# Five more edge groups of a graph kernel sorted in its first stage (60 of 202 instead of 55), two in every second block

## The reference

```python
# L0: twice
agg = segment_sum(x[src], dst) / max(count, 1)
h = relu(agg @ W_l + b_l + x @ W_r)
# then
x = layernorm(x + h @ W_out + b_out)
# L1: over the edges
out = concatenate([x[src], edge_attr], axis=1)           # 206250 x 128
out = selu(out @ W1a + b1a) @ W1b + b1b
mean = segment_sum(out, dst) / max(count, 1)
h = concatenate([x, mean, u[batch]], axis=1)
x = layernorm(x + selu(h @ W2a + b2a) @ W2b + b2b)
```

## Time and profile before

| | us |
|---|---|
| median of 3 runs | 3514.62 |
| lowest, highest | 3498.83, 3517.24 |
| profiled execution | 3513.92 |
| its span, first to last instruction | 3512.1 |
| mean granted TensorE clock | 0.782 |

### The profile page before, as it was taken

The page is one execution under the profiler, slowest core; times in us unless marked ns, Lnnn a source line. Parts: engine busy times, 40 slices in busy tenths (PEclk is TensorE's granted clock), DMA queues, the critical chain, the costliest instruction groups (busy, mean ns, idle before and its releaser), DMA issues.

```text
span 3512.1 us, 52018 instructions
## 1 busy us (share of the span) xinstructions
PE 2340.6 (67%) x18382; PEld 1666.3 (47%) x18382; DVE 1547.9 (44%) x3098; ACT 1005.2 (29%) x2255; POOL 1824.9 (52%) x1853
## 2 busy tenths in 40 slices
PE   3999999787888862565656566565656656564643
PEld 1555565444444431454544455454545545453543
DVE  6899998233333441333433333343333334332333
ACT  4778776000000011222222222222222222222222
POOL 6366763555455557454444545444554544455552
PEclk9999999888888875677777777777767777676566
DMA  6658877649455521322222222222222222221111
GB/s 227 196 196 241 224 210 253 175 119 219 143 173 176 176 68 40 83 48 44 46 48 43 48 46 48 44 46 48 43 48 46 48 44 46 48 42 42 39 37 34
DMA packets 478172, 346.45 MB, mean 99 GB/s; under 512 B 357844, under 2 KB 428687, under 8 KB 474253
## 3 DMA queue, kind: packets, MB, share of 16 engines
q1 hardware_dynamic: 367443, 272.49, 27.4%
q0 software_dynamic: 54240, 57.23, 7.5%
q10 hardware_dynamic: 56250, 13.52, 1.9%
HBM read 200.58 MB, written 142.39 MB: 98 GB/s over the span
## 4 chain that ended last, share of the span: by engine, by line
PE 36%; another core or an unknown queue 25%; issue 22%; DVE 6%; ACT 5%; DMA 2%; SPq 2%; DVEq 1%; ACTq 1%; POOL 0%; POOLq 0%
PE agg_ps L1533 5%; PE u_ps L1664 4%; PE cnt_ps L1404 4%; PE cnt_ps L1625 3%; PE agg_ps L1410 3%; PE agg_ps L1411 3%; PE u_ps L1660 2%; PE agg_ps L1674 2%; PE agg_ps L1633 2%; ACT A_sb L1071 2%; PE t_ps L1617 1%; PE v_ps L1650 1%; DVEq L2192 1%; ACT A_sb L1217 1%
## 5 line engine op out<-in xcount | busy, mean ns | idle before, releaser
L976 POOL DMA_INDIRECT A_sb<-source_terms,src_cur x1172 | 1118.5, 954 | 1048.4 <-ACT src_cur L1203 718.1
L927 POOL DMA_INDIRECT sorted_edges<-pm_row,pm_to x440 | 482.7, 1097 | 338.8 <-DVE pm_to L1981 215.5
L1664 PE MATMUL u_ps<-arena 128*128 128x64 bf16 x3399 | 253.4, 212 | 385.5 <-issue 385.2
L1533 PE MATMUL agg_ps<-A_sb,arena 128*128 128x448 f16 x1911 | 426.1, 373 | 68.7 <-issue 65.7
L1857 DVE TENSOR_TENSOR arena<-iota_code,arena 128x2048 f16<-128x2048 f16 (+1 forms) x392 | 438.3, 1186 | 33.5 <-PE cnt_ps L1404 31.2
L1071 ACT ACTIVATE A_sb<-cnt_ps 128x392 f32 (+1 forms) x784 | 386.0, 499 | 123.4 <-PE cnt_ps L1404 73.0
L1664 PEld LDWEIGHTS u_ps<-arena 128*128 128x128 bf16 x3399 | 196.7, 110 | 439.9 <-issue 431.9
L2194 DVE TENSOR_TENSOR A_sb<-A_sb,agg_ps 65x48 f32 (+1 forms) x290 | 78.0, 269 | 728.7 <-remote 624.4
L1533 PEld LDWEIGHTS agg_ps<-A_sb,arena 128*128 128x128 bf16 x1911 | 189.5, 101 | 274.0 <-issue 133.0
L1404 PE MATMUL cnt_ps<-arena 128*128 128x98 f16 x3136 | 282.2, 214 | 31.2 <-ACT A_sb L1071 23.2
L1633 PE MATMUL agg_ps<-A_sb 128*65 128x48 f32 x2344 | 210.9, 250 | 131.4 <-issue 73.4
(11 more groups left out here) (308 smaller groups left out, 3379.3 us busy)
## 6 DMA issues: line engine op xcount, KB each, us to landing
counts_matrix<-A_sb SPq DMA_DIRECT2D x14, 5488.0 KB
A_sb<-counts_matrix SPq DMA_DIRECT2D x12, 5488.0 KB
arena<-in_edge_attr_dram SPq DMA_DIRECT2D x96, 256.0 KB
sorted_edges<-zrow SPq DMA_DIRECT2D x11, 1716.0 KB
A_sb<-source_terms,src_cur POOLq DMA_INDIRECT x1172
arena<-sorted_edges SPq DMA_DIRECT2D x143, 128.0 KB
overlapping_rows<-A_sb SPq DMA_DIRECT2D x1, 13056.0 KB, 39.4
A_sb<-in_edge_attr_dram SPq DMA_DIRECT2D x50, 256.0 KB
```

Of the source, the lines that this page charges most:

```text
L927: pool.indirect_dma_start(out=sorted_d, out_offset=bass.IndirectOffsetOnAxis(ap=pm_to[:, k, j:j + 1], axis=0), in_=pm_row[:, k, j, :], in_ ...
L976: pool.indirect_dma_start(out=gath[k][:, j * F:(j + 1) * F], out_offset=None, in_=p_d, in_offset=bass.IndirectOffsetOnAxis(ap=src_cur[k][: ...
L1533: ins = pe.matmul(agg_ps[:, 0:SBN], Hsb[:, part, blk, :], Asb(half)[:, blk, :], start=False, stop=(part == 2), skip_group_check=True)
L1664: ins = pe.matmul(u_ps[:, j * F:(j + 1) * F], lane_p[u % 2][:, a, j * P:(j + 1) * P], P3[:, 2 * b + a, part, :], start=False, stop=(part = ...
```

## The change

`NR` goes from 11 to 12: 12 ranges, 60 sorted groups, 156 units, 142 conventional groups. `IN_STAGE1` goes from 10 to 15: blocks 4, 6, 8, 10 and 12 (`TWO_SORTS`) sort two groups each, blocks 3, 5, 7, 9 and 11 one. The second group of a block is started on VectorE when the one-hots up to group 32 are made and the first group's slots are found; TensorE places it after group 32 (the first after 16), and its slots are found when the one-hots up to group 48 are made. SyncE loads the groups a block ahead, so two in a block ahead of a double one. Three ranges are cleared before block 2 instead of two; the nine later clears stay where they were. GpSimd waits for all three before the first scatter. `LAST_STEP` goes from 121 to 116, so the 156 + 3 steps of units lie in slots 4 to 115: 47 slots with two, 65 with one. The last 26 slots are as before. The number of groups sorted between the stages and in stage 2 is the same, 5 and 40, at the same places. The units' products stay in three bf16 parts.

```diff
--- before.py
+++ after.py
@@ -69,7 +69,7 @@
 DEEP = 6
 
 RG = 5
-NR = 11
+NR = 12
 PG = RG * NR
 NEGC = NEG - PG
 CELL = 2 * P
@@ -80,10 +80,11 @@
 BEFORE = 3 * (NSB - 1) + 3 - PG
 UNIT_RING = 3
 FIRST_SORT = 3
-IN_STAGE1 = 10
+TWO_SORTS = (4, 6, 8, 10, 12)
+IN_STAGE1 = 10 + len(TWO_SORTS)
 SOONER = IN_STAGE1 + 5
-PLACE_AT = 16
-SLOT_AT = 32
+PLACE_AT = (16, 32)
+SLOT_AT = (32, 48)
 TOTALS = 4 * -(-NEG // 4)
 
 
@@ -112,7 +113,7 @@
 UNIT_RANGE = [r for r, tiles in enumerate(CELL_TILES) for _ in range(sum(tiles) // UT)]
 STEPS = UNITS + 3
 FIRST_STEP = 4
-LAST_STEP = 121
+LAST_STEP = NEGC - 26
 
 FIN_SLOT = LAST_STEP + 1
 FIN_ORDER = list(range(4, 12)) + [0, 1, 2, 3] + list(range(12, NSB))
@@ -533,10 +534,13 @@
             eng.wait_ge(row_stored, 16 * (NSB + 1))
 
         def placed(q):
-            return cnt_ps[q % 2][:, 0:NCELL] if IN_STAGE1 <= q < SOONER else t_ps[:, SBN:SBN + NCELL]
+            return cnt_ps[(q - IN_STAGE1) % 2][:, 0:NCELL] if IN_STAGE1 <= q < SOONER else t_ps[:, SBN:SBN + NCELL]
 
         def sorted_in(s):
-            return [s - FIRST_SORT] if FIRST_SORT <= s < FIRST_SORT + IN_STAGE1 else []
+            if not FIRST_SORT <= s < NSB - 1:
+                return []
+            first = s - FIRST_SORT + sum(t < s for t in TWO_SORTS)
+            return [first, first + 1] if s in TWO_SORTS else [first]
 
         def fin_stage(h, stage):
             n = h - FIN_SLOT - stage
@@ -600,9 +604,12 @@
                     sp.dma_start(xm[:, 1 - half, :, :], by_node(x, s - 1)).then_inc(xm_in[1 - half], 16)
                 if s >= 2:
                     store_h(s - 2, half)
-                    load_group(s - 2)
+                    for q in sorted_in(s + 1):
+                        load_group(q)
+                if s == NSB - 2:
+                    load_group(IN_STAGE1)
                 if s == NSB - 1:
-                    for q in range(s - 1, IN_STAGE1 + PRING):
+                    for q in range(IN_STAGE1 + 1, IN_STAGE1 + PRING):
                         load_group(q)
                 sp.wait_ge(counts_moved, (s + 1) * SB_GROUPS + 2)
                 sp.dma_start(A_d[bass.ds(s, 1), :, :].rearrange("a p n -> (a p) n"), A_sb[:, half, :]).then_inc(A_stored[half], 16)
@@ -617,15 +624,15 @@
                 sp.dma_start(pm_dst[:, :], dst[0:PG * EG].rearrange("(r q) -> r q", q=RG * EG)[:, 0].partition_broadcast(P)).then_inc(pm_dst_in, 16)
             superblock(0, 0)
             superblock(1, 1)
-            for r in range(2):
+            for r in range(IN_STAGE1 // RG):
                 blank(r)
             for s in range(2, NSB):
                 superblock(s, s % 2)
                 if s >= FIRST_SORT + 1:
                     if s == FIRST_SORT + 1:
                         sp.wait_ge(pm_gone[0], 16 * EJ)
-                    if s - FIRST_SORT + 1 < NR:
-                        blank(s - FIRST_SORT + 1)
+                    if s - FIRST_SORT - 1 + IN_STAGE1 // RG < NR:
+                        blank(s - FIRST_SORT - 1 + IN_STAGE1 // RG)
             sp.wait_ge(xT_ready, NSB - 2)
 
             def last_rows(rows, done):
@@ -934,7 +941,7 @@
                     gather_fine((m + 3) * SETS, (m + 4) * SETS)
                 split_h(m - 2)
                 if m == FIRST_SORT:
-                    pool.wait_ge(pm_blank, PM_BLANK + 32)
+                    pool.wait_ge(pm_blank, PM_BLANK + 16 * (IN_STAGE1 // RG))
                 for q in sorted_in(m):
                     scatter(q)
             pool.wait_ge(rows_ready, NSB)
@@ -1420,8 +1427,8 @@
                         turn_first(1)
                     if k == (LATE_TURN if known and s == 0 else 3 * BG) - 1 and (not known or s < NSB - 1):
                         turn_windows(s + 1)
-                    if k == PLACE_AT:
-                        for q in sorted_in(s):
+                    for q, at in zip(sorted_in(s), PLACE_AT):
+                        if k == at:
                             place_group(q)
                     if known and s == 0:
                         continue
@@ -1880,15 +1887,16 @@
                 if not known or s < NSB - 2:
                     dve.wait_ge(fine_in, 16 * SETS * (s + 3))
                     find_windows(s + 2)
-                for q in sorted_in(s):
+                for q, at in zip(sorted_in(s), SLOT_AT):
                     sort_group(q)
-                    make_hot(s, half, begun, SLOT_AT)
-                    begun = SLOT_AT
-                    own_terms(s - 2)
+                    make_hot(s, half, begun, at)
+                    begun = at
+                    if at == SLOT_AT[0]:
+                        own_terms(s - 2)
                     slot_group(q)
                 if s >= 2 and not sorted_in(s):
-                    make_hot(s, half, begun, SLOT_AT)
-                    begun = SLOT_AT
+                    make_hot(s, half, begun, SLOT_AT[0])
+                    begun = SLOT_AT[0]
                     own_terms(s - 2)
                 make_hot(s, half, begun, SB_GROUPS)
 

```

## The result

The kernel after takes 3641.4 us (median of 4 runs, 3630.3 to 3650.7) against 3515.9 for the kernel before beside it: 1.036 times, 95% interval 1.030 to 1.042. That is slower, by 125 us, and outside the predicted range of 3500 to 3553. Its profiled execution has a span of 3647.4 us, 135.3 more than the one of before.

| stretch | before | after | change | forecast |
|---|---|---|---|---|
| start to the end of counting (stage 1) | 602.3 | 658.0 | +55.7 | +23 |
| from there to slot 4 (stage 2 and what joins on) | 798.8 | 794.5 | -4.3 | 0 |
| slots with units (117, 112) | 1793.4 | 1887.5 | +94.1 | -10 in all of stage 3 |
| the last slots and the end | 317.7 | 307.5 | -10.2 | |

A forecast was written before the change was run, and what follows sets the result against it. It took TensorE and VectorE to bound stage 1 together, and stops with no engine full to mark stage 3. From 3513.9 us, +14 (sorts), +9 (clear) and -10 (stage 3) gave 3527 us, range 3500 to 3553.

The forecast's parts named there:

- (b): Stage 1, SyncE's queue: a third clear before block 2 delays the load of `xm` and adds 9 us, bounds 0 to 10.1.
- (a): Stage 1, VectorE: a second sort makes each double block 3.0 us longer, 14 us in all, bounds 10.6 to 19.3.
- (c): Stage 1, GpSimd: eight more scatters per double block take 15.7 us and fit in 16.4 us of waiting per pair.
- Cost 0: Stage 1, GpSimd: the added scatters, with later windows and a later split of h, were to add no time.
- Rival 2: Stage 1: runs of 16 scatters stop the engines, up to 25 us, so 3552 us; chance 0.2.
- added nothing: Stage 1, block 2: no time was charged for what a longer wait for `xm` does to the granted clock.
- I take the stops as a cost of the gathers, so of the conventional groups: Stage 3: engine stops, 53% of the chain or 8.1 us a slot, were charged to conventional groups, not units.
- b: Stage 3: time of one unit, 3.3 us, beside a, a slot without its units, 11.3; change -5a + 13b = -13.6.
- My way by slots: Stage 3: double slots of 18.6 us and single ones of 14.3 gave +5.9 us, a second unit costing 4.3.
- two ways that charged a slot with 11.3 and 12.0: Stage 3: splits by the chain and by the slots without units, giving changes of -13.6 and -24.6 us.
- rival 3: Stage 3: the stops belong to units, so it changes by +38 us and the kernel takes 3575; chance 0.05.
- No engine is full there: Stage 3, slots with units: GpSimd, the busiest but TensorE, has only 884.71 of 1793.41 us of work.

The follow-up runs named there:

- after_again: The kernel after, run once more unchanged, on a chip without stops: 2615.1 us against 2632.5 for the kernel before, ratio 0.9924.
- sort_doubles: The kernel after without the second groups' scatters in stage 1 and with the 47 double slots first, on a chip with stops: 3495.4 us against 3486.2 for the kernel before.
- scatter_only: The kernel before with 8 more scatters into a scratch table in blocks 4, 6, 8, 10 and 12, on a chip without stops: 2639.0 us against 2638.2.
- paused forms: Kernels before and after with seven small memsets behind each group's gathers in stage 3 (before also paused in stage 2): unit slots 1716.7 and 1753.0 us.
- before_paused: The kernel before with seven small memsets behind every group's gathers in stage 3, on a chip with stops: 3329.3 us against 3486.2, ratio 0.956.
- two_two: The kernel after with its double slots in pairs (2 2 1 1 1) instead of alternating, on a chip without stops: unit slots 1123.3 us.

## Why the prediction was wrong

**Right.** (b), the clear: 9 us forecast, 8.7 measured (14 by the base of another chip). (a), VectorE: double blocks of 41.6 forecast; 41.0 to 42.5 in after_again, and 41.6, 41.6, 42.8, 41.5 and 45.9 in sort_doubles. (c) in its sum: 40 scatters cost GpSimd's own time nothing. Beside VectorE's one-hots a scatter did take longer: of the 55 of scatter_only between 255 and 525 us, the 44 that lay mostly beside one took 1.69 us on average, the 11 others 0.96. Where no stop disturbs, stage 1 grew by 25.0 us, and by 32.6 on another chip, against 23. Stage 2: none, and measured -4 and 0.

**Stage 1, wrong by 33 us.** The step that failed is "Cost 0" in (c). Rival 2 named the cause, runs of 16 scatters; I priced it with stage 2's 5.1 us a block in five blocks and gave it 0.2. The scatters alone, on a chip with stops, cost 36 us. They don't stop all engines here, as rival 2 had it (1.5 us in all): ScalarE and TensorE stand for some 2 us at a time while VectorE works on. Two more things were missing. A run goes on over the end of its block, since the next block's window gathers are behind it without a gap (20 in a row), so the next, single block suffers: the single blocks have 29 us of the 56, where I gave them nothing. And there were stretches at 1.2 GHz (0.85 in the window shown), 37.5 us of them between 230 us and the end of counting, where the trace before has none and after_again 10.2. I had looked at this for `xm` only and "added nothing". How the 56 us divide into waits and clock I can't say.

**Stage 3, wrong by 94** (84 us more where 10 less were forecast; the slots with units alone 94 more). The step that failed is "I take the stops as a cost of the gathers, so of the conventional groups". Cost of gathers they are, but not so much each: a run of 8 costs 3.1 us of all engines' time, a run of 16 not 6.2 but 10.3 to 11.2. The number of runs of 16 comes with short slots. In the kernel after a single slot of 5.5 us behind a double one frees two buffers at once, and GpSimd then does both groups' gathers in one run; in the kernel before the run begins in the second of two single slots of about 10 us. I read one cycle of four slots, with one such run in it, and shared its stops out among the groups in equal parts; the change gives 38 such runs instead of 29, with five groups fewer. How much of the 94 us this is, two ways tell. In the first two traces themselves the idle time of all engines grew by 62 us and TensorE's busy time by 40 (1083.37 in the earlier trace rows, 1123.70 after), together 102, near the 94. Against their paused forms the two kernels lost 134.5 and 76.7 us, a difference of 58. This second way is weak: the paused forms ran beside another base (3511.7 us for the kernel before, where the first result has 3515.9), and with before_paused's 1660.9 from yet another chip the difference would be 2.

The other 36 us, the growth of the paused kernels on one chip, are the size of b, 3.3 us forecast and 5.7 found in the paused kernels. My way by slots gave +5.9 and a second unit 4.3 us, the nearest; I averaged it with two ways that charged a slot with 11.3 and 12.0. The price of rival 3 (b = 6.0, a = 8.0, +38) was near (36 in the paused kernels) by luck: the stops are not the units', for the unit products' idle time fell from 471 to 67 us with the units all there. A slot without units lasts 11.6 us, not 7.7 (after, 290.0 us for 25), so "a times slots plus b times units" is itself only a rough form here.

**What no row could have shown** is that the kernel has another bound on a chip without stops. There stage 3 is GpSimd's chain of gathers, units are free, and five groups less give 50 us; with 25 lost in stage 1 that leaves 25, where scatter_only's and after_again's spans differ by 24 and the medians by 17. "No engine is full there" was true of the trace and not of the kernel.

**The versions.** Both kernels are beaten, on a chip with stops, by the kernel before with the pauses in stages 2 and 3 (3273.8 us). The same pauses, with the double slots first, cost 19% on a chip without stops, where the kernel after is the best that was run, with two_two level.

## What to carry to other kernels

Before you give a stop a price per instruction, sort the stops by the length of the run they fall in: two runs of eight and one of sixteen held the same gathers and cost 6 and 10 us. Ask of any schedule change which releases it brings together, above all on the queue whose runs cost more than in proportion. And when half of a chain is "issue", the trace shows a condition of that chip and not only the kernel: say what bounds the kernel without it, and forecast both. And take the base of a small difference from the same chip: the kernel before, with the same pauses, had slots with units of 1660.9 and 1716.7 us on two chips.

## What the hardware showed that I had not expected

With stops, back-to-back indirect transfers of GpSimd (1.25 us apart) hold up TensorE, VectorE and ScalarE together from about 8.6 us into the run of gathers shown, while GpSimd itself keeps its pace; without stops the 1132 gathers of after_again went out in one run, and in the 1122 us of its unit slots all three stood for 3.9 us. In the trace before a gap of 3.0 us ended a run's effect and one of 1.1 us did not (a run of 8 behind it had 3.4 to 3.8 us in stage 2, against 0.6 on average). In stage 1, with VectorE's one-hots beside them, the same long runs held up ScalarE and TensorE but hardly ever all three. The same kernel took 2632 or 3512 us, with a mean granted clock of 0.88 or 0.78; the stops and the lower clock are the differences that the traces show, not what causes them.
